# One decoder layer on one core: where the FFN's squares are summed, how the first two groups' stacks are filled, and where the down weights lie

## The reference, cut to what matters

```python
# attention: 16 heads of 32, softmax, plus a small "splat" term
q = heads(x @ Wq); k = heads(x @ Wk); v = heads(x @ Wv)
attn = softmax(q @ k.T / sqrt(32));  std = (attn @ v) @ Wo
# ssm: for 16 states n, over 512 steps:
state = state * exp(delta * A[n]) + delta * u * B[n];  y += state * C[n]
# ffn: ternary weights, 2048 hidden channels
gate, up = split(x @ wq_gu.T);  h = silu(gate) * up
hn = h * rsqrt(mean(h * h, axis=-1) + eps)
out = hn @ wq_p.T
```

## Time and profile before

| | us |
|---|---|
| median of 3 runs (1515.85 to 1525.48) | 1517.29 |
| the profiled execution | 1519.1 |
| its span, from first to last instruction | 1516.6 |
| PE busy | 1194.1 |
| DVE busy | 1245.1 |
| ACT busy | 759.7 |
| POOL busy | 214.6 |

### The profile page before, as it was taken

The page is one execution under the profiler, slowest core; times in us unless marked ns, Lnnn a source line. Parts: engine busy times, 40 slices in busy tenths (PEclk is TensorE's granted clock), DMA queues, the critical chain, the costliest instruction groups (busy, mean ns, idle before and its releaser), DMA issues.

```text
span 1516.6 us, 14134 instructions
## 1 busy us (share of the span) xinstructions
PE 1194.1 (79%) x4565; PEld 560.5 (37%) x4570; DVE 1245.1 (82%) x1485; ACT 759.7 (50%) x1110; POOL 214.6 (14%) x247
## 2 busy tenths in 40 slices
PE   4673748677788987887988797887898887887896
PEld 3342313222244542332344443333344533333453
DVE  5877988988879998778789997888889996887434
ACT  6765434435366643636566632555476633552231
POOL 1000122001111123200111122101111132001101
PEclk8755978888879998979989998899799998888898
DMA  6853687456338869544239869434159777452132
GB/s 190 273 174 121 146 213 181 104 119 139 65 100 210 240 145 221 144 113 98 64 91 235 220 159 239 105 85 111 50 143 248 171 195 194 98 129 59 49 98 69
DMA packets 113688, 220.17 MB, mean 145 GB/s; under 512 B 15584, under 2 KB 26336, under 8 KB 113616
## 3 DMA queue, kind: packets, MB, share of 16 engines
q1 hardware_dynamic: 94240, 151.25, 33.8%
q0 software_dynamic: 18432, 67.12, 23.0%
q10 hardware_dynamic: 944, 0.92, 0.2%
HBM read 122.37 MB, written 29.62 MB: 100 GB/s over the span
## 4 chain that ended last, share of the span: by engine, by line
DVE 39%; PE 30%; issue 10%; ACT 5%; DMA 4%; POOL 1%; SPq 1%; DVEq 0%; ACTq 0%; POOLq 0%
DVE ST L876 14%; DVE ST L868 6%; PE ps L1467 5%; PE ps L1285 5%; DVE MX L932 5%; PE ps L1268 4%; PE ps L1420 3%; PE ps L1349 2%; PE ps L1436 2%; DVE ST L879 2%; PE ps L1377 2%; DVE RD L1081 2%; DVE QAK L1096 2%; DMA qk_parts<-PT 2%; PE ps L1236 1%
## 5 line engine op out<-in xcount | busy, mean ns | idle before, releaser
L876 DVE TENSOR_TENSOR_SCAN ST<-dA,ST 128x1024 f32<-128x1024 f32 x128 | 312.6, 2442 | 8.8 <-ACT dA L579 6.0
L1467 PE MATMUL ps<-V,GU 128*128 128x512 f16 x1024 | 240.3, 390 | 5.6 <-DVE V L1063 5.6
L473 POOL DMA_DIRECT2D YA<-ST x128 | 111.0, 867 | 945.0 <-DVE ST L879 887.0
L932 DVE TENSOR_REDUCE MX<-ps 128x1 f32<-128x512 f32 x256 | 165.1, 686 | 84.7 <-PE ps L1268 84.0
L579 ACT ACTIVATE dA<-DL,Aneg 128x511 f32<-128x511 f32 x256 | 168.4, 713 | 82.4 <-DVE ST L876 82.1
L711 ACT ACTIVATE PT<-ps 128x1024 f32<-128x1024 f32 x128 | 126.3, 1021 | 119.0 <-PE ps L1377 118.2
L1268 PE MATMUL ps<-KS,QS 96*128 96x512 f32 x256 | 127.6, 560 | 74.1 <-DVE MX L932 42.3
L1436 PE MATMUL ps<-WP,QS 128*128 128x512 f32 x512 | 144.8, 427 | 29.5 <-DMA WP<-proj_tiles 21.7
L879 DVE TENSOR_TENSOR ST<-ST,BC 128x1024 f32<-128x1024 f32 x128 | 159.4, 1246 | 4.4
L868 DVE TENSOR_TENSOR ST<-DU,BC 128x1024 f32<-128x1024 f32 x128 | 155.8, 1217 | 7.3 <-DMA BC<-bc_rows 7.3
L1467 PEld LDWEIGHTS ps<-V,GU 128*128 128x128 bf16 x1024 | 97.6, 100 | 136.5 <-issue 27.3
(11 more groups left out here) (230 smaller groups left out, 1593.9 us busy)
## 6 DMA issues: line engine op xcount, KB each, us to landing
YA<-ST POOLq DMA_DIRECT2D x128, 512.0 KB, 7.2
BC<-bc_rows SPq DMA_DIRECT2D x64, 512.0 KB, 6.1
qk_parts<-PT SPq DMA_DIRECT2D x64, 256.0 KB, 4.3
GU<-gu_tiles SPq DMA_DIRECT2D x64, 256.0 KB, 8.5
WP<-proj_tiles SPq DMA_DIRECT2D x64, 256.0 KB, 7.3
QS<-qk_parts SPq DMA_DIRECT2D x96, 128.0 KB, 3.4
KS<-qk_parts SPq DMA_DIRECT2D x96, 128.0 KB, 3.8
ST<-in_L_ffn_w_gate_up_dram SPq DMA_DIRECT2D x16, 256.0 KB, 3.4
```

What stands on the lines that cost most here:

```text
L876: nc.vector.tensor_tensor_scan(flat, dA[:, a, :, :].rearrange("p e s -> p (e s)"), flat, 0.0, ALU.mult, ALU.add).then_inc(s_scan, 1)
L932: nc.vector.tensor_reduce(MX[:, j % 2, qt, h:h + 1], ps[:, n % 2, :], AX_X, ALU.max).then_inc(s_mx, 1)
L1467: last = mm(ps[:, f % F_RING, :], GU[:, t % GU_RING, k, m * P:(m + 1) * P], XHL[:, z, k, :], start=(k == 0 and z == 0), stop=(k == KT - 1 ...
```

## The change

Three edits.

1. **Squares.** ACT squares all 16 tiles, into a ring of eight places in `PT`. PE sums them: after the down products of tiles 3, 7, 11 and 15, `square_sums` issues four products of 32 columns of ones, one for each tile of the group, into the four column quarters of bank 3, which accumulates over the four groups. At the end ACT copies bank 3 to `RD`, and the four products of L1480 follow as before; each sum is now held 32 times, and the factor of L1102 says so. DVE's 15 additions and POOL's square are gone.
2. **Stacks of groups 0 and 1.** Units 0 to 3 are no longer written to DRAM. `move_part` copies each part from `QKP` into its blocks of the stacks by DMAs of 32 partitions, one per head and block: 8 for the high part and 4 for the low part, 12 a unit, 48 a batch. 8 writes and 24 loads a batch are gone. ACT's L675 and POOL's L487 of units 2 to 5 wait on the moves of unit u-2. Groups 2 and 3 are as before.
3. **Down weights.** `WP` is `QS[0]`, a ring of four, and each tile is asked for two tiles earlier than before.

```diff
+WP_RING = 4
-POOL_SQUARES = 1
+SQ_GROUP = 4
-        SQ = [QAK[:, 4, :], PT[:, 1, 0, :]]
+        SQ = [PT[:, i // HG, i % HG, :] for i in range(2 * SQ_GROUP)]
-        WP = sb("WP", [P, 2, H], F32R)
+        WP = QS[0]
+        HI_ROWS, LO_ROWS = ((0, 1), (0, 2)), ((2,), (1,))
+        def wait_unit_moved(engine, b, u):
+            j, z = UNITS[u]
+            if j < 2:
+                for pair in range(HG // 2):
+                    engine.wait_ge(s_stack[j][pair], 288 * b + 96 * (z + 1))
+            else:
+                engine.wait_ge(s_part[u % 2], 64 * b + 32 * (u // 2 - 1))
# SP, attention_phase
+            def move_part(u, part, rows):
+                j, z = UNITS[u]
+                for h in range(HG):
+                    for r in rows[z]:
+                        sp.dma_start((QS, KS)[z][j][D * r:D * r + D, h, :].bitcast(F32),
+                                     QKP[D * h:D * h + D, 2 * part + u % 2, :].bitcast(F32)).then_inc(s_stack[j][h // 2], 16)
                 for u, (j, z) in enumerate(UNITS):
                     sp.wait_ge(s_hi, 2 * NG * b + u + 1)
-                    sp.dma_start(qk_parts[b, z, 0, ...], QKP[:, u % 2, :]...).then_inc(s_part[u % 2], 16)
+                    if j < 2:
+                        move_part(u, 0, HI_ROWS)
+                    else:
+                        sp.dma_start(qk_parts[b, z, 0, ...], ...)
                     sp.wait_ge(s_lo, 2 * NG * b + u + 1)
...
-                    if u in (2, 3):
-                        load_stack(b, j)
                     load_next_bc(b, fill_halves(2 * KT + u, first))
# SP, ffn_phase
+                def load_wp(t):
+                    if t >= WP_RING:
+                        sp.wait_ge(s_dn, NT * b + t - WP_RING + 1)
+                    sp.dma_start(WP[:, t % WP_RING, :].bitcast(F32), proj_tiles[t]).then_inc(s_wp[t % WP_RING], 16)
                 for t in range(GU_RING - 1):
                     load_gu(t)
+                sp.wait_ge(s_s, 2 * KT * NG * b + 2 * KT * (NG - 1))
+                for t in range(WP_RING // 2):
+                    load_wp(t)
                 for t in range(NT):
-                    if t >= 2:
-                        sp.wait_ge(s_dn, NT * b + t - 1)
-                    sp.dma_start(WP[:, t % 2, :].bitcast(F32), proj_tiles[t]).then_inc(s_wp[t % 2], 16)
+                    if t + WP_RING // 2 < NT:
+                        load_wp(t + WP_RING // 2)
# POOL and ACT, unit u >= 2 (one each)
-                        pool.wait_ge(s_part[u % 2], 32 * KT * b + 32 * (u // 2))
+                        wait_unit_moved(pool, b, u - 2)
# ACT, ffn_phase
                 def square(t):
-                    if t >= POOL_SQUARES:
-                        act.wait_ge(s_acc, NT * b + max(t - 1, POOL_SQUARES))
-                        nc.scalar.square(SQ[t % 2], HT[:, t % 2, :]).then_inc(s_sqa, 1)
+                    if t >= 2 * SQ_GROUP:
+                        act.wait_ge(s_ssq, NT // SQ_GROUP * b + t // SQ_GROUP - 1)
+                    nc.scalar.square(SQ[t % (2 * SQ_GROUP)], HT[:, t % 2, :]).then_inc(s_sqa, 1)
...
                 if not last:
                     x_transposed(b + 1)
+                act.wait_ge(s_ssq, NT // SQ_GROUP * (b + 1))
+                nc.scalar.copy(RD[:, :], ps[:, 3, :]).then_inc(s_acc, 1)
# DVE, low_of_product
-                        nc.vector.tensor_tensor(RD[:, :], RD[:, :], SQ[t % 2], ALU.add).then_inc(s_acc, 1)
# PE
+            def square_sums(b, g):
+                pe.wait_ge(s_sqa, NT * b + SQ_GROUP * (g + 1))
+                for i in range(SQ_GROUP):
+                    t = SQ_GROUP * g + i
+                    last = mm(ps[D * i:D * i + D, 3, :], ones[:, :], SQ[t % (2 * SQ_GROUP)],
+                              start=(g == 0), stop=(t + SQ_GROUP >= NT), tile_position=(0, D * i))
+                last.then_inc(s_ssq, 1)
                     if t > 0:
                         down(b, t - 1)
+                    if t > 0 and t % SQ_GROUP == 0:
+                        square_sums(b, t // SQ_GROUP - 1)
-                pe.wait_ge(s_acc, NT * (b + 1))
+                pe.wait_ge(s_acc, b + 1)
                 for r in range(KT):
                     last = mm(ps[:, 3, r:r + 1], RD[:, r * P:(r + 1) * P], ones[:, 0:1], start=True, stop=True)
```

More of the change, by code:

```diff
@@ L156, in decoder_layer @@
         s_gu = [sem(f"s_gu{i}") for i in range(GU_RING)]
-        s_wp = [sem(f"s_wp{i}") for i in range(2)]
-        s_gp, s_up, s_sg, s_h, s_hh, s_hl, s_sq, s_sqa, s_acc, s_dn = (sem(n) for n in (
-            "s_gp", "s_up", "s_sg", "s_h", "s_hh", "s_hl", "s_sq", "s_sqa", "s_acc", "s_dn"))
+        s_wp = [sem(f"s_wp{i}") for i in range(WP_RING)]
+        s_gp, s_up, s_sg, s_h, s_hh, s_hl, s_sqa, s_ssq, s_acc, s_dn = (sem(n) for n in (
+            "s_gp", "s_up", "s_sg", "s_h", "s_hh", "s_hl", "s_sqa", "s_ssq", "s_acc", "s_dn"))
         s_rms, s_ms, s_inv, s_r3, s_out = (sem(n) for n in ("s_rms", "s_ms", "s_inv", "s_r3", "s_out"))
@@ L341, in load_stack @@
                 i = j % 2
[L342 to L348, removed]
+                sp.wait_ge(s_s, 2 * KT * NG * b + 2 * KT * (j - 1))
                 for pair in range(HG // 2):
@@ L367, in attention_phase @@
                 for u, (j, z) in enumerate(UNITS):
+                    if b == 0 and u == 1:
+                        sp.wait_ge(s_wst[1], 16 * NT)
                     sp.wait_ge(s_hi, 2 * NG * b + u + 1)
-                    sp.dma_start(qk_parts[b, z, 0, P * j:P * j + P, :], QKP[:, u % 2, :].bitcast(F32)).then_inc(s_part[u % 2], 16)
+                    if j < 2:
+                        move_part(u, 0, HI_ROWS)
+                    else:
+                        sp.dma_start(qk_parts[b, z, 0, P * j:P * j + P, :], QKP[:, u % 2, :].bitcast(F32)).then_inc(s_part[u % 2], 16)
                     sp.wait_ge(s_lo, 2 * NG * b + u + 1)
-                    sp.dma_start(qk_parts[b, z, 1, P * j:P * j + P, :], QKP[:, 2 + u % 2, :].bitcast(F32)).then_inc(s_part[u % 2], 16)
-                    if u in (2, 3):
-                        load_stack(b, j)
+                    if j < 2:
+                        move_part(u, 1, LO_ROWS)
+                    else:
+                        sp.dma_start(qk_parts[b, z, 1, P * j:P * j + P, :], QKP[:, 2 + u % 2, :].bitcast(F32)).then_inc(s_part[u % 2], 16)
                     load_next_bc(b, fill_halves(2 * KT + u, first))
@@ L514, in ffn_phase @@
                             add_y_behind(b + 1, n, a)
-                    if t < POOL_SQUARES:
-                        pool.wait_ge(s_h, NT * b + t + 1)
-                        if t > 0:
-                            pool.wait_ge(s_acc, NT * b + t)
-                        dst = RD[:, :] if t == 0 else SQ[0]
-                        nc.gpsimd.tensor_tensor(dst, HT[:, t % 2, :], HT[:, t % 2, :], ALU.mult).then_inc(s_sq, 1)
-                        pool.wait_ge(s_sq, POOL_SQUARES * b + t + 1)
-                        if t == 0:
-                            pool.sem_inc(s_acc, 1)
-                        else:
-                            nc.gpsimd.tensor_tensor(RD[:, :], RD[:, :], SQ[0], ALU.add).then_inc(s_acc, 1)
                 if not last:
@@ L706, in attention_phase @@
                             else:
-                                act.wait_ge(s_part[0], 32 * KT * (b + 1))
-                                act.wait_ge(s_part[1], 32 * KT * (b + 1))
+                                act.wait_ge(s_part[0], 64 * (b + 1))
+                                act.wait_ge(s_part[1], 64 * (b + 1))
                             bank = score_bank(b, j, 2 * p)
@@ L1077, in low_of_product @@
                                             HL[:, t % 2, :].bitcast(F32), ALU.subtract).then_inc(s_hl, 1)
-                    if t >= POOL_SQUARES:
-                        dve.wait_ge(s_sqa, (NT - POOL_SQUARES) * b + t - POOL_SQUARES + 1)
-                        dve.wait_ge(s_acc, NT * b + t)
-                        nc.vector.tensor_tensor(RD[:, :], RD[:, :], SQ[t % 2], ALU.add).then_inc(s_acc, 1)
                 for t in range(NT + 1):
@@ L1101, in ffn_phase @@
                 dve.wait_ge(s_rms, b + 1)
-                nc.vector.tensor_scalar(VE[:, :], ps[:, 3, 0:KT], 1.0 / HID, RMS_EPS, ALU.mult, ALU.add).then_inc(s_ms, 1)
+                nc.vector.tensor_scalar(VE[:, :], ps[:, 3, 0:KT], 1.0 / (HID * D), RMS_EPS, ALU.mult, ALU.add).then_inc(s_ms, 1)
                 dve.wait_ge(s_inv, b + 1)
```

16 lines of the change are left out of this document (7 added, 9 removed).

## The result

| | before | after |
|---|---|---|
| median, us | 1518.35 (4 runs, 1515.85 to 1525.48) | 1541.15 (4 runs, 1539.81 to 1543.16) |
| the profiled execution | 1519.1 | 1541.1 |
| its span | 1516.6 | 1539.1 |
| DVE busy | 1245.1 | 1197.1 |
| PE busy | 1194.1 | 1214.5 |

The changed kernel takes 1.0143 times as long as before, interval [1.0120, 1.0166]. I had forecast 1497 us, range 1486 to 1510. DVE is busy 48 us less, some 41 of them the 60 additions, and yet the span is 22.5 us longer.

A forecast was written before the change was run, and what follows sets the result against it. DVE was taken as the bound in FFNs 0 to 2 and the Q and K units, PE in batch 3's FFN. Terms -27.5 + 1.0 + 4.2 + 2.5 - 5.0 + 4.5 = -20.3 us gave a median of 1497.0 us, range 1486 to 1510.

The forecast's parts named there:

- The step that failed: Units of batches 1 to 3: SP issues 24 moves at 0.47 us each, 11.3 us, the last at about 588.1.
- 12 x 0.47 = 5.6 us: Batch 0: time of group 0's 12 stack loads ahead of BC on SP's queue, expected to go.
- predicted +1.5: Batches 1 to 3: the scan behind ACT's L675 starts 2.7 us late, less 1.2 of stretching; +4.5 us in all.
- Rival (c): SP's queue: each move holds it for about 1 us, making the kernel slower than before, 1540 us; chance 0.07.
- turning point: SP's queue: the kernel becomes slower than before from about 0.82 us a move, 0.35 above 0.47.
- (b): SP's queue: moves go out more slowly, at 0.62 us each, giving 1510 us; chance 0.12.
- Batch 0, -5.0: Batch 0's units: DVE's 6.80 us wait for BC shrinks to 0.6, less 1.2 of scan stretching; bounds -7 and 0.
- Squares, -27.5: FFNs of batches 0 to 2: 45 DVE additions go at 0.61 us each; DVE tile 6.40 to 5.79 us.
- The cover on PE: FFNs of batches 0 to 2: PE needs 5.55 us a tile against DVE's 5.79, hiding square products by 0.24.
- Batch 3, +4.2: Batch 3's FFN, PE-bound: three square groups at 0.88 us, 2.6, plus a 1.6 us tail, uncovered.
- DMA backlog, +2.5: FFNs of batches 0 to 2: W-reloading tiles need 6.28 us of DMA, above 5.79; YA additions land late, +2.5 us in all.
- Down weights, 0: FFN: the ring of four removes PE's 6.8 us of waits a batch, none on the path, so worth 0.

The follow-up runs named there:

- `moves_halved`: The changed kernel with each move cut into two of 256 columns, 24 DMAs of 32 KB a unit: 1636.82 us, one execution.
- `bc_first`: Changed kernel with stacks through DRAM again, four gate and up tiles, and SP's BC load ahead of the twelve stack loads: 1503.74 us, 0.987 of before.
- `last_by_dve`: `bc_first` with DVE adding the squares in the last batch, as in the kernel before: 1498.30 us, 0.9839 of before.

## Why the prediction was wrong

**The step that failed** is the one that priced SP's queue: "24 x 0.47 = 11.3 us", with the pitch of the stack loads. Those carry 128 KB out of DRAM; the moves go from SBUF to SBUF and are issued 0.63 us apart by the median, 0.80 on the mean in batch 1. 24 of them took 19.1 us. Even for the loads 0.47 was the pitch of the quiet ones: in the trace before, the 12 loads of group 0 take 205.25 to 212.78 us in batch 0 and 587.00 to 594.96 in batch 1, 0.63 and 0.66 each, with the long issues in them. So the "12 x 0.47 = 5.6 us" of batch 0 was 7.5 in its own trace, and the mean over a whole burst would have given 24 x 0.66 = 15.9 us for the moves. Unit 2 was out of `QKP` at 598.2 where I had 591.6, and the scan at place 12 started at 600.09 against 590.73: 9.4 us late, for which I had 2.7, less the 1.2 of its stretching. To the first maximum that made +10.3 us a batch, predicted +1.5: 26.4 of the 42.8 us between my -20.3 and the span's +22.5. My own formula with the right pitch, 1.5 + 24 x 0.33 = 9.4, would have come near. Batch 0 took 8.9 of the rest (below), the FFNs 3.8, and the scores of batches 1 to 3 another 3.7, for which I had nothing.

**The rivals.** Rival (c)'s 1540 us came true, its price did not, so that number is luck: it asked for about 1 us a move, 38 us, where 0.80 makes 24. The 14 us between are made up by batch 0's and the other scores, the FFNs, and 2.6 us more before the first maxima. Its turning point was wrongly worked out. If batch 0's 5.0 us are lost, only 15.3 are left to be eaten up, not 25.3: 15.3 / 72 = 0.21 above 0.47, so the kernel turns slower at 0.68 us a move and not at 0.82. Between the 0.62 of (b) and that point lay 0.06 us, and I gave the slower side 0.07. `moves_halved` shows the steepness by itself: 36 DMAs, 21.5 us a batch.

**Batch 0, -5.0.** The mechanism (BC behind twelve loads) was right, and `bc_first` shows it. But the twelve moves of unit 2 lie ahead of BC too. I counted four of them at 0.47, but SP was still behind with units 0 and 1, and BC left at 214.09, later than the 212.78 of before. The wait stayed, 7.20 us. Even freed of it, the kernel gives back two thirds within the first group's scores in `bc_first`, and all by the FFN in `last_by_dve`, which no sentence of mine had.

**Squares, -27.5.** Right: the DVE tile is 5.80 us (I had 5.79), 45 x 0.60 us. The cover on PE held once the weights came in time, and an undisturbed FFN gained 8.9 of its 9.0 us, so that the tail in batches 0 to 2 cost 0.1 us each, not 0.3. **Batch 3, +4.2:** measured 4.9. The group cost 1.08 us in the loop, not the 0.88 that I drew from its row of 1.04, and the tail 2.0 against 1.6. `last_by_dve` got back 5.4 us by the medians, 5.2 in its trace.

**DMA backlog, +2.5.** Of the right kind, +5.8 measured, but through another door: not by the landing of YA, which I had followed, but by one late gate tile a batch in batches 0 and 1, the first of which took 12.4 us to land, in a ring of three. **Down weights, 0:** by the traces 5 us, for the same reason.

**The landing of a move.** For a 64 KB move the trace has 2.0 us at least and 2.7 by the median of all (4.3 into `QS`, 2.0 into `KS`), against the 2.3 which I estimated from the Trainium skill, "SBUF — State Buffer"; I had taken 3.5 from the stack loads. For `KS`, to which unit 2 belongs, the Trainium skill was nearer, for `QS` my value. It was beside the point, since the queue and not the landing set the time. Of the advice in the Trainium skill, "SBUF — State Buffer", The DMA setup-cost knee, to use 128 partitions and the largest single transfers, these runs bear out the second half: halving the moves cost 96 us, halving the loads 47. The Trainium skill gives the fixed time of a transfer as the reason; here it was the issue on the queue. No run varies the partitions. I had the advice in the text and gave it no term.

## What to carry to other kernels

Before a store and reload is replaced by direct moves, count the DMAs that one queue has to issue in the stretch, and multiply by the mean pitch of that kind of DMA over a whole burst, long issues included: here 8 writes and 24 loads became 48 moves, and batches 1 to 3 lost 31 us by it. Where the kind isn't in the trace, its range has to reach well above the nearest kind, and the sum has to be run again at its upper end with all that is queued behind. An engine that waits for a buffer should first do what others wait for. And a shorter tile makes old rings too short: after 0.6 us was saved, a fourth gate tile and the ring of four for the down weights were needed to keep it.

## What the hardware showed unexpectedly

- SBUF-to-SBUF moves of 32 partitions hold SP's queue for 0.59 us at 64 KB and at 32 KB alike, loads from DRAM of the same shape for 0.42 us.
- Two queues issue such moves side by side, at medians of 0.59 to 0.77 us each; the 48 moves of a batch then leave in 31.0 us for 39.2, and land in 4.7 us for 2.7 by the median.
- Among several moves or loads in a row, single issues take 1.2 to 2.0 us. In the changed kernel all 32 such moves start 1.3 to 3.6 us after POOL began to issue an accumulating DMA, and 32 of the 40 moves that start there are such. That the one brings the other isn't shown.
- Four products with 32 columns of ones at full precision, in the column quarters of one bank, cost 1.08 us in a PE-bound loop, a little more than the length of their row (1.00 to 1.04).
